# Three TensorE semaphore rises per expert tile in place of seven, in a routed attention and mixture-of-experts block

## The reference

```python
h = _layernorm(x, axis=-1) * (1 + ca) + sa
x = x + ga * _L0_attn_ref(h, wq, wk, wv, wo)
h = _layernorm(x, axis=-1) * (1 + cb) + sb
...
scores = softmax(h @ Wr + br);  top 2 of the 8 experts;  weights = softmax of the two scores
hid = gelu(h @ W1[e] + b1[e])            # 128 -> 512
expert_out = hid @ W2[e] + b2[e]         # 512 -> 128
x = x + gb * sum of weight * expert_out over the two experts
```

## Time and profile before

| | us |
|---|---|
| median of three runs | 1108.02 (1107.33 to 1108.35) |
| the profiled execution, its own time | 1111.02 |
| its span | 1109.2 |
| PE busy in the span | 1020.6 (92%) |
| ACT busy | 970.1 (87%) |
| DVE busy | 926.9 (84%) |
| POOL busy | 823.0 (74%) |

### The profile page before, as it was taken

One profiled execution on the slowest core, in us unless ns is written; L12 is line 12 of the kernel. 1 busy time (PEld: TensorE's weight loads), 2 busy tenths in 40 slices (PEclk: granted clock), 3 DMA queues, 4 the chain that ended last, 5 costly groups with the idle time before them and its releaser, 6 DMA issues. The chain is left out here.

```text
span 1109.2 us, 27344 instructions
## 1 busy us (share of the span) xinstructions
PE 1020.6 (92%) x7434; PEld 791.5 (71%) x7434; DVE 926.9 (84%) x2710; ACT 970.1 (87%) x3515; POOL 823.0 (74%) x1193
## 2 busy tenths in 40 slices
PE   5799999999999999999999999999989999999700
PEld 3488888888888888888888888888865555579600
DVE  5888899998999999888888888888766997778737
ACT  5899999999999999999999999999769999999433
POOL 3656568888888888888878788888745687877744
PEclk9899999999999999999999999999999999999955
DMA  5410000000100000000000000000034233321157
GB/s 152 126 34 24 14 16 26 23 23 26 35 25 26 23 26 13 16 15 18 13 16 14 15 14 16 16 16 13 19 111 125 86 118 104 95 88 38 48 208 255
DMA packets 53704, 57.90 MB, mean 52 GB/s; under 512 B 7964, under 2 KB 42639, under 8 KB 53556
## 3 DMA queue, kind: packets, MB, share of 16 engines
q1 hardware_dynamic: 36468, 35.10, 10.7%
q0 software_dynamic: 8640, 16.87, 4.3%
q10 hardware_dynamic: 8448, 4.20, 1.3%
HBM read 33.08 MB, written 23.97 MB: 51 GB/s over the span
## 5 line engine op out<-in xcount | busy, mean ns | idle before, releaser
L741 ACT ACTIVATE squares<-unit 128x128 f32<-128x128 f32 x1024 | 273.0, 302 | 8.4 <-PE unit L1196 8.4
L563 POOL TENSOR_TENSOR roped<-roped,rope_b 128x512 f32<-128x512 f32 x128 | 170.1, 1329 | 90.1 <-DVE rope_b L1087 88.2
L741 ACT ACTIVATION_READ_ACCUMULATOR squares<-unit 128x1 f32 x1024 | 233.9, 235 | 0.0
L1070 DVE TENSOR_TENSOR roped<-unit,cos_sb 128x512 f32<-128x512 f32 x256 | 174.4, 681 | 32.9 <-ACT squares L741 31.6
L1548 POOL DMA_INDIRECT y_rows<-y_out,place_y x142 | 156.1, 1099 | 53.5 <-issue 40.3
L1087 DVE TENSOR_TENSOR rope_b<-unit,sin_sb 128x512 f32<-128x512 f32 x256 | 174.2, 681 | 0.0
L719 ACT ACTIVATE probs<-scores,rr 128x256 f32<-128x256 f32 x256 | 123.8, 483 | 51.5 <-issue 25.5
L1276 PEld LDWEIGHTS unit<-ident,roped 128*128 128x128 f32 x1024 | 118.0, 142 | 30.9 <-ACT k_t L758 12.3
L1039 DVE SCALAR_TENSOR_TENSOR acc<-pv,den,acc 128x128 f32<-128x128 f32 x448 | 139.0, 341 | 0.4
L1276 PE MATMUL unit<-ident,roped 128*128 128x128 f32 x1024 | 135.4, 275 | 0.6 <-POOL roped L563 0.5
L571 POOL TENSOR_TENSOR roped<-roped,rr 128x1024 f32<-128x1024 f32 x64 | 121.6, 1900 | 9.6 <-DVE roped L1096 8.8
(11 more groups left out here) (310 smaller groups left out, 2973.6 us busy)
## 6 DMA issues: line engine op xcount, KB each, us to landing
shared<-y_rows SPq DMA_DIRECT2D x16, 512.0 KB, 5.6
x_all<-in_L_attn_x SPq DMA_DIRECT2D x32, 128.0 KB, 2.2
h_late<-in_L_ffn_W SPq DMA_DIRECT2D x16, 256.0 KB, 3.5
out_x<-hidden ACTq DMA_DIRECT2D x16, 256.0 KB, 2.6
rope_b<-x_rows SPq DMA_DIRECT2D x13, 258.0 KB
tile_x<-x_rows SPq DMA_DIRECT2D x12, 258.0 KB, 3.5
y_rows<-y_out,place_y POOLq DMA_INDIRECT x142, 2.3
ga_b<-mod_dram SPq DMA_DIRECT2D x32, 64.0 KB, 3.0
```

The source lines that it names most:

```text
L563: pool.tensor_tensor(out=roped[parity][:, u, heads], in0=roped[parity][:, u, heads], in1=rope_b[:, u % 2, heads], op=ALU.add).then_inc(S[" ...
L741: nc.scalar.activation(squares[:, c * D:(c + 1) * D], UN[0][:, c * D:(c + 1) * D], ACT.Square, accum_out=ssq[parity][:, u * H + c:u * H + ...
L1070: nc.vector.tensor_tensor(out=roped[parity][:, u, heads].rearrange("p (g c) -> p g c", c=D // 2), in0=UN[0][:, heads].rearrange("p (g c) - ...
```

## The change

In the expert stage PE raises one semaphore, `turn_done`, in place of `t_done`, `down_done` and `back_done`. It rises with the last transpose into `XT` of every body and, in the last five bodies, with the last instruction of the body. A value of it therefore says that PE has begun body n and done the transposes at its head, and with them all of body n-1. `up_done` rises after every second chunk. The waits are translated by three new functions:

```diff
+        def x_turned(i):
+            return i + 1
+        def down_ended(i):
+            return i + 5 if i >= 0 else 0
+        def y_turned(i):
+            return i + 6 if i >= 0 else 0
@@ ACT
-                    wait(act, "down_done", i + 1)
-                    wait(act, "back_done", i - 1)
+                    wait(act, "turn_done", max(down_ended(i), y_turned(i - 2)))
...
-                    wait(act, "t_done", i + 1)
+                    wait(act, "turn_done", x_turned(i))
...
-                        wait(act, "up_done", FC * n + k + 1)
+                        wait(act, "up_done", FC // 2 * n + k // 2 + 1)
...
-                            wait(act, "down_done", n - RING + 1)
+                            wait(act, "turn_done", down_ended(n - RING))
@@ DVE
-                    wait(dve, "down_done", i + 1)
-                    wait(dve, "back_done", i - 1)
+                    wait(dve, "turn_done", max(down_ended(i), y_turned(i - 2)))
...
-                    wait(dve, "back_done", i + 1)
+                    wait(dve, "turn_done", y_turned(i))
@@ PE
-                    ins.then_inc(S["t_done"], 1)
+                    ins.then_inc(S["turn_done"], 1)
...
-                        ins.then_inc(S["up_done"], 1)
+                        if k % 2:
+                            ins.then_inc(S["up_done"], 1)
...
-                    ins.then_inc(S["down_done"], 1)
...
-                    ins.then_inc(S["back_done"], 1)
+                if n + 2 >= NT:
+                    ins.then_inc(S["turn_done"], 1)
```

More of the change, by code:

```diff
@@ L256, in adaln_block @@
             ex_hi_done ex_split b_in tile_in0 tile_in1 tile_in2 tile_in3 tile_in4 tile_in5
-            places_ready t_done x_hi_done x_split up_done gelu_done hid_hi_done hid_split down_done y_cols_done back_done y_step
+            places_ready turn_done x_hi_done x_split up_done gelu_done hid_hi_done hid_split y_cols_done y_step
             y_stored0 y_stored1 y_stored2 y_stored3 y_stored4 y_stored5 back_in0
```

## The result

| | before | after |
|---|---|---|
| median of 20 runs each, on the same chips, us | 1108.73 (1107.01 to 1110.28) | 1111.01 (1108.06 to 1112.8) |
| ratio, with its 95% interval | | 1.0017 (1.0010 to 1.0023) |
| profiled execution, own time / span | 1111.02 / 1109.2 | 1110.95 / 1109.1 |

The ratio makes 1.9 us (1.1 to 2.5), slower; the two medians stand 2.3 us apart. At 0.17% it is inside the 0.2% that the prediction took as the limit of measurement, though its interval reaches 0.23%. The forecast was 1110.0 us, +1.95.

A forecast was written before the change was run, and what follows sets the result against it. The stage looked bound by PE at 6.06 us per tile, its end by POOL's scatters from tile 31 on. PE's 1.30 plus ACT's and DVE's 0.65 gave +1.95 on 1108.02: 1110.0 us, range 1107.9 to 1112.4.

The forecast's parts named there:

- Rises cost PE nothing: PE's up and down products: 139 fewer rises were to save at most 0.5 us, taken as 0.
- The wait of `gelu` for chunk 1: ACT in each tile: `gelu` starts 0.65 us later, a shift against PE paid once, not a loss per tile.
- `down_done` folded: ACT's `y_cols` waits for the transposes; `gelu` could start at 911.55, before 911.85, so 0.65 us remains, not 1.4.
- `back_done` folded, 0: DVE's `y_pos` waits for four more transposes, 0.44 us, but ACT's last `hid_hi` comes later: 0.
- The early stalls: PE before its steady pace: tile 4's down product +0.65, then the transposes at 885.02 another 0.65, PE +1.30.
- The sum: `y_out` of tile 31: PE's 1.30 plus ACT's and DVE's 0.65, +1.95; the end +1.60 to +1.95.
- POOL pinned to the `hid_lo` pairs: Around 951 us DVE's `hid_lo` pairs hold up POOL's scatters, four taking one tile's time, so POOL follows at +1.95.
- The slack of 0.35: POOL at tile 31: first scatter 1.12 us after `y_out` ends, against 0.77 at tile 4, so 0.35 us of slack.
- the upper bound: Last scatter at tile 31's end of the chain: +1.95 taken, from bounds of 1.60 and 1.95.
- POOL's phase: Rival: scatters meeting `hid_lo` cost up to 0.53 us more, 1.1 to 2.9 us on top, 1111.1 to 1112.9; chance 0.33.
- Absorbed: Rival: one or both early PE stalls don't follow; 1109.2 with one, 1108.5 with neither; chance 0.20.
- Faster by the rises: Rival: rises cost PE 0.026 us each, hidden from the trace; the end at 1105.6 to 1107; chance 0.05.

The follow-up runs named there:

- e3: Kernel before with a rise on each matmul of the up and down products, 736 more, nobody waiting for them: 1108.24 us, ratio 0.9995.
- e5: Kernel before with `up_done` rising in pairs only from body 14 on: 1109.60 us, ratio 1.0001.
- e6: Kernel before with `up_done` rising once per tile, after chunk 3: 1118.20 us, ratio 1.0078.
- e1: Kernel before with only the `up_done` rises in pairs, the other three semaphores kept: 1111.03 us, ratio 1.0019.
- e2: Changed kernel with `up_done` after every chunk again, so only `turn_done` replaces the three semaphores: 1108.85 us, ratio 1.0000.
- e4: Kernel before with `up_done` rising in pairs only in bodies 0 to 13: 1110.53 us, ratio 1.0013.
- e7: Changed kernel with DVE's `y_pos` and `y_out` ahead of the second `hid_lo` pair from body 28 on: 1110.39 us, ratio 1.0017 to the kernel before.
- e8: Changed kernel with `hid_lo` as `hidden` times zero, one SBUF input in place of two: 1106.55 us, ratio 0.9981 to the kernel before.
- e9b: Kernel before with `y_pos` and `y_out` ahead of the second `hid_lo` pair from body 3 on, run again in another set: 1107.12 us, ratio 0.9986.

## Why the prediction was right

**Rises cost PE nothing: right.** After shows 2.59 us for both products; e3 shows it with sixteen rises more per large tile.

**The wait of** `gelu` **for chunk 1, +0.65, paid once: right.** 2.03 us from the transposes in place of 1.39, the tile at 6.06. e5 has the term by itself (+0.72, PE 0.00). e6 gives the limit of "once".

`down_done` **folded: right.** It is under the other delay (e1 equals after), and alone, in e2, ACT's part is 0.30 against 0.35 worked out.

`back_done` **folded, 0: not contradicted**, and not tried alone; e2, which holds both folds, leaves `y_out` of tile 31 at +0.31 with 0.24 of it PE's; of the 0.07 left e3, which folds nothing, has 0.06.

**The early stalls: the first right, the second wrong.** The step that failed is "PE is at +0.65 and would wait until 885.02 + 1.30: PE +1.30". DVE was to reach its `x_lo` 1.30 later because it has no idle time in those bodies and the same work. It has the same instructions, but they did not take the same time. DVE's timelines ahead of `x_lo` of the earlier trace rows, of the kernel before:

```profile
882.47 0.38 DVE L1829 TENSOR_SCALAR big_i<-tiles_i 128x8 int32<-128x8 int32 x1
...
883.71 0.43 DVE L1836 CAST big_f<-big_i 128x8 f32<-128x8 int32 x1
```

and of the kernel after:

```profile
883.35 0.21 DVE L1840 TENSOR_SCALAR big_i<-tiles_i 128x8 int32<-128x8 int32 x1
...
884.01 0.33 DVE L1844 TENSOR_SCALAR tiles_i<-tiles_i 128x8 int32<-128x8 int32 x1
...
884.58 0.17 DVE L1847 CAST big_f<-big_i 128x8 f32<-128x8 int32 x1
```

`big_i` and `big_f` took 0.81 us together before and 0.38 after, the instruction between them (0.17 before) 0.33: 0.27 us less in all. The three long ones start well inside a scatter, 0.55 to 0.65 us after its start (at 881.88 and 883.16 before, at 883.36 after); `big_i` and `big_f` of after start just ahead of one (883.36 and 884.65), and the one of 0.17 us before starts only 0.14 us into one. That POOL is what stretched them is read from this timing and not tried by a run of its own. Another phase between the two engines is another sum. The prediction weighed that for POOL and not for DVE. `x_lo` came 1.01 late and PE with it, and the stall at 903.73 gave 0.08 back. The term measured +0.28 in place of +0.65 (e1 +0.94 in all, e4 +0.96: the same again in three kernels).

**The sum.** PE 0.92, ACT and DVE 0.65, together 1.57, and with the 0.07 that e3 has too, 1.64; `y_out` of tile 31 came at +1.65 where +1.95 was forecast. **POOL pinned to the** `hid_lo` **pairs: right around 951**, with +1.58 as the sum now says, **but it does not decide the end.** The slack of 0.35 was not used in after (distance 1.21), and was in e1, e3, e4 and e5 (0.77). e4 is pinned in the same tiles and still uses it, for one scatter in tile 30. The same DVE timeline thus allows two ends 0.3 us apart. The prediction took the upper bound because of the pinning, and that this bound fitted after was luck. Whether it is the kernel or the execution that picks the end stays open: each kernel has one profiled execution.

**The rivals.** *POOL's phase*: POOL lost 0.09 us more than `y_out` up to tile 31, and it decides from 0.35. The sign that the prediction named for it, a distance beyond 1.12 us at tile 31, is there (1.21), but by no more than that 0.09. The mechanism is real (e7, e8, e9b), and on the way, in tile 30, it had POOL at +2.33; at the end the change had set off next to nothing of it. *Absorbed*: one of the two stalls did follow in full, the other in part; the +1.64 lies between this rival and the forecast, nearer to the forecast. *Faster by the rises*: ruled out by e3.

The absolute time, 1111.01, stands 1.0 above the forecast, since the kernel before was at 1108.73 beside it and not at the 1108.02 of three runs. That is 0.7 of it. The rest goes against the trace, in which the last scatter moved less than forecast, and lies within the scatter of the medians.

## What to carry to other kernels

A semaphore rise on a stream of large matmuls was free here, and waiting for a coarser one was not: each consumer is late by the work between the two rises. Price such a change by asking, first, whether the consumer's own round has room (then it is a shift, paid once, and not a loss per round), second, where a producer has waited for that consumer (there the shift becomes the producer's time), and third, who reads the result last. And when one engine runs at the pace of another without ever waiting for it, look for what ties them: here four scatters and two overlaps made exactly one tile, and moving `y_out` between the pairs of `hid_lo` loosened the knot and moved the last scatter of after by more than the rises had (1.98 us back, against 1.64).

## What the runs showed of the hardware

**DVE and POOL can stretch each other.** A scatter took 0.98 us alone and mostly up to 1.51 us where it met `hid_lo`, a tensor-tensor instruction with both inputs in SBUF; one, at 904.20 in the kernel before, met four of these instructions in a row and took 2.72 us, more than the prediction's "up to 0.53 us more". Beside `y_pos` and `y_out`, which read one input from PSUM, it took 0.98 (e9b at 951.37, above). An overlap alone costs nothing: of the 126 scatters from tile 4 on in the kernel before 75 overlapped `hid_lo`, and 35 of these took under 1.00 us. All of the 40 longer ones, and all 40 of after, had `hid_lo` running 0.12 us after their start, the 0.12 us that the prediction found at 951.12 and 952.93; 12 more in each kernel had it too and were no longer for it. The other way round, DVE's instructions on 8 columns took 0.33 to 0.43 us in place of 0.17 to 0.21. The Trainium skill (SBUF — State Buffer, "Who interferes with whom") says that a tensor-tensor with both inputs in SBUF contends with GpSimd's reads and, by inference, leaves the generation of descriptors alone. The first half agrees with the rows (1.50 us at 952.29 in after); an indirect scatter, which also reads row numbers (`place_y`), is not left alone.

**The clock is part of the scatter between executions.** Windows of 3 us at the start of the expert stage, of the kernel before and of e3; the number ahead of the DMA share is the granted clock:

```profile
833.00:836.00 3.00, 3.00 (x9) 1.04 (x8) 3.00 (x7) 2.83 (x5) 1.11 (x1) 0.51 0.60 181
```

```profile
833.00:836.00 3.00, 3.00 (x18) 1.64 (x16) 2.73 (x6) 3.00 (x5) 2.05 (x2) 1.00 0.34 96
```

At 0.51, about 1.2 GHz of 2.4, PE ran 9 matmul instructions in the window where it ran 18 at full clock. In both executions PE had just stood still for 2.90 us, ahead of the transposes at 831.71 before and at 830.47 in e3, so that idle time alone does not tell the two apart. The execution of e3 (and that of e2) had no such stretch and reached body 4 1.68 us earlier, counted from the start of the stage. With one profiled execution of each kernel no run shows what decides it; it is as large as the whole effect studied here.
